# Attention value products: one accumulator over two banks in 64x32 tiles of TensorE, in place of two accumulators in 128x32 tiles

## What is computed

```python
q = (x @ Wq.T + bq).reshape(B, M, H, dqk)      # B 8, M 1024, H 8, dqk 2
k = (x @ Wk.T + bk).reshape(B, M, H, dqk)
v = (x @ Wv.T + bv).reshape(B, M, H, dv)       # dv 16
scores = jnp.einsum('bmhd,bnhd->bhmn', q, k) / math.sqrt(dqk)
scores = jnp.where(scores >= 0, scores, 0.2 * scores)
beta = jax.nn.softmax(scores, axis=-1)
out = jnp.einsum('bhmn,bnhd->bmhd', beta, v).reshape(B, M, C)
```

## Time and profile before

| | |
|---|---|
| median of three runs | 942.72 us |
| lowest, highest | 940.2 us, 944.03 us |
| span of the profiled execution, first to last instruction | 940.0 us |
| PE matmuls, busy | 861.2 us (92%) |
| DVE, busy | 735.3 us (78%) |
| ACT, busy | 691.3 us (74%) |
| GpSimd, busy | 601.5 us (64%) |
| granted TensorE clock, mean | 0.981 of full |

### The profile page before, as it was taken

How to read it: one execution, slowest core, us unless ns; L and a number is a source line. 1 busy time by engine, 2 the same in 40 slices (tenths; PEclk the granted TensorE clock), 3 DMA queues, 4 the chain that set the end, 5 groups by cost and what they waited for, 6 DMA issues and landing times. The chain is left out here.

```text
span 940.0 us, 20061 instructions
## 1 busy us (share of the span) xinstructions
PE 861.2 (92%) x7499; PEld 348.9 (37%) x7500; DVE 735.3 (78%) x859; ACT 691.3 (74%) x811; POOL 601.5 (64%) x610
## 2 busy tenths in 40 slices
PE   0688269999999999999999999999999999999997
PEld 0444112222222224776867732222222222222222
DVE  5788889999999994101011099999999999999996
ACT  0578888888888887444453568888888888888886
POOL 3355247777777663999999226657567575765782
PEclk9999659999999999999999999999999999999999
DMA  7833101111111112233242210102112111210202
GB/s 214 303 66 74 32 27 33 51 40 51 47 27 36 25 38 88 90 121 116 93 138 71 94 44 22 40 19 59 36 25 59 25 36 29 70 29 13 69 18 55
DMA packets 71225, 59.36 MB, mean 63 GB/s; under 512 B 33770, under 2 KB 58178, under 8 KB 71136
## 3 DMA queue, kind: packets, MB, share of 16 engines
q1 hardware_dynamic: 61520, 48.06, 17.6%
q0 software_dynamic: 8192, 9.37, 3.6%
q10 hardware_dynamic: 1424, 0.76, 0.3%
HBM read 31.58 MB, written 30.02 MB: 66 GB/s over the span
## 5 line engine op out<-in xcount | busy, mean ns | idle before, releaser
L1133 DVE TENSOR_SCALAR ps<-ps 128x1024 f32<-128x1024 f32 x512 | 600.1, 1224 | 14.6 <-PE ps L825 11.7
L718 ACT ACTIVATE pr<-ps 128x1024 f32<-128x1024 f32 x512 | 523.4, 1023 | 104.5 <-PE ps L835 72.9
L855 PE MATMUL ps<-pr,vp 128*32 128x256 f32 x4096 | 327.2, 392 | 0.1
L835 PE MATMUL ps<-q,kz 64*128 64x512 bf16 x1024 | 200.7, 389 | 10.2 <-DVE ps L1133 4.4
L825 PE MATMUL ps<-q,kz 62*128 62x512 bf16 x1024 | 200.3, 389 | 2.9 <-DMA q<-parts_dram 1.3
L505 POOL DMA_INDIRECT xs<-eout,idxs x128 | 129.0, 1008 | 105.0 <-ACT pr L718 75.5
L490 POOL DMA_INDIRECT disp<-xn,idx x128 | 125.9, 984 | 50.8 <-issue 29.2
L835 PEld LDWEIGHTS ps<-q,kz 64*128 64x128 bf16 x1024 | 49.0, 93 | 225.7 <-DVE ps L1133 188.4
L1152 DVE TENSOR_TENSOR pr<-ps,parts 128x1024 f32<-128x1024 f32 x12 | 14.7, 1225 | 149.6 <-PE ps L920 149.6
L855 PEld LDWEIGHTS ps<-pr,vp 128*32 128x32 f32 x4096 | 81.1, 108 | 119.4 <-issue 117.6
L744 ACT ACTIVATE pr<-ps,b1s 128x512 f32<-128x512 f32 x96 | 65.8, 687 | 53.7 <-PE ps L909 53.7
(11 more groups left out here) (122 smaller groups left out, 530.3 us busy)
## 6 DMA issues: line engine op xcount, KB each, us to landing
moved<-att SPq DMA_DIRECT2D x480, 8.0 KB
disp<-pr SPq DMA_DIRECT2D x12, 512.0 KB, 4.9
eout<-pr SPq DMA_DIRECT2D x12, 512.0 KB, 2.9
y<-in_x SPq DMA_DIRECT2D x8, 512.0 KB, 8.1
out<-y SPq DMA_DIRECT2D x7, 512.0 KB
w<-in_w1t SPq DMA_DIRECT2D x12, 256.0 KB, 3.2
w<-in_w2t SPq DMA_DIRECT2D x12, 256.0 KB, 3.4
xs<-disp SPq DMA_DIRECT2D x6, 512.0 KB, 4.9
```

What stands on the lines that cost most here:

```text
L718: act.activation(pr[:, c % BUFS, 2 * pair:2 * pair + 2, :], ring[i % RING], ACT.Exp, scale=SLOPE).then_inc(S["exps"], 1)
L835: last = pe.matmul(ring[i % RING][:, k, :], kz[r:r + TILE, hg, pair, kc * P:(kc + 1) * P], q2[r:r + TILE, hg, qh * HALF:(qh + 1) * HALF], ...
L855: last = pe.matmul(acc[p % 2][32 * g:32 * g + 32, cols], vp[:, hg, kc, g, :], pr[:, c % BUFS, g % PAIRS * 2 + g // PAIRS, cols], start=(kc ...
L1133: dve.tensor_scalar(s, s, 0.0, 1.0 / SLOPE - 1.0, ALU.max, ALU.mult).then_inc(S["relu"], 1)
```

## The change

The value products go over two row tiles. `values(m)` is called once for each unit as before, but it now issues eight matmuls in tiles of 64 rows and 32 columns: four heads for keys 0 to 63 of the block, and four heads for keys 64 to 127. The two row tiles work on different halves of the columns, and so write into different banks: the lower keys into the bank of half `m % 2`, the upper keys into the other one; the next call takes the crossed halves. The accumulator is therefore one for all passes, half of each of banks 6 and 7 (256 columns each). `pv` counts every call, and the counts of the waits on it are doubled. Every call waits for the one before it (`pv` of m), and the first call of pass p waits until pass p - 1 (not p - 2) is turned. TURN goes from 5 to 4. `scores` and `shifted` keep their 64x128 tiles. The PE's transposes at the end of a stretch go into `out_t`, the whole of bank 6.

```diff
-TURN = 5
+TURN = 4
...
-        acc = [ps[:, 2 * RING + k, :] for k in range(2)]
+        acc = ps[:, 2 * RING:2 * RING + 2, 0:HALF // 2]
+        out_t = ps[:, 2 * RING, :]
...
-                act.copy(ot[:, p % 2, :], acc[p % 2]).then_inc(S["acc_evac"], 1)
+                act.copy(ot[:, p % 2, :].rearrange("p (a q) -> p a q", a=2), acc).then_inc(S["acc_evac"], 1)
...
-            def values(c, half):
+            def values(m):
+
+                c, half = divmod(m, PAIRS)
 
                 p, kc = divmod(c, TB)
                 hg = p // NQ % NHG
-                cols = slice(half * HALF // 2, (half + 1) * HALF // 2)
-                pe.wait_ge(S["exps"], PAIRS * (c + 1))
+                if half == 0:
+                    pe.wait_ge(S["exps"], PAIRS * (c + 1))
+
+                wait_done(pe, "pv", PAIRS * c + half)
...
-                    wait_done(pe, "turned", p - 1)
-                for g in range(HG):
-                    last = pe.matmul(acc[p % 2][32 * g:32 * g + 32, cols], vp[:, hg, kc, g, :],
-                                     pr[:, c % BUFS, g % PAIRS * 2 + g // PAIRS, cols],
-                                     start=(kc == 0 and half == 0), stop=(kc == TB - 1), tile_position=(0, 32 * g),
-                                     skip_group_check=True)
-                if half:
-                    last.then_inc(S["pv"], 1)
+                    wait_done(pe, "turned", p)
+                for k in range(2):
+                    r, a = TILE * k, (k + half) % 2
+                    cols = slice(a * HALF // 2, (a + 1) * HALF // 2)
+                    for g in range(HG):
+                        last = pe.matmul(acc[32 * g:32 * g + 32, a, :], vp[r:r + TILE, hg, kc, g, :],
+                                         pr[r:r + TILE, c % BUFS, g % PAIRS * 2 + g // PAIRS, cols],
+                                         start=(kc == 0 and half == 0), stop=(kc == TB - 1),
+                                         tile_position=(r, 32 * g), skip_group_check=True)
+                last.then_inc(S["pv"], 1)
...
-                dve.wait_ge(S["pv"], TB * (p + 1))
+                dve.wait_ge(S["pv"], UP * (p + 1))
                 if p > 1:
                     dve.wait_ge(S["att_rdy"], quotients(p - 2))
-                dve.transpose(ot[:, p % 2, :], acc[p % 2]).then_inc(S["turned"], 1)
+                dve.transpose(ot[:, p % 2, :].rearrange("p (a q) -> p a q", a=2), acc).then_inc(S["turned"], 1)
```

More of the change, by code:

```diff
@@ L365, in _ @@
             spread(BH * NPB - 2)
-            sp.wait_ge(S["pv"], BH * NPB * TB)
+            sp.wait_ge(S["pv"], BH * NPB * UP)
             load_expert(1, 1)
@@ L425, in value_rows @@
                 if b > 0:
-                    pool.wait_ge(S["pv"], TB * (pass_at(b - 1, hg, NQ - 1) + 1))
+                    pool.wait_ge(S["pv"], UP * (pass_at(b - 1, hg, NQ - 1) + 1))
                 pool.tensor_copy(vp[:, hg, :, :, 0:DV1],
@@ L706, in evacuate @@
             def evacuate(p):
-                act.wait_ge(S["pv"], TB * (p + 1))
+                act.wait_ge(S["pv"], UP * (p + 1))
                 act.wait_ge(S["att_rdy"], quotients(p - 2))
-                act.copy(ot[:, p % 2, :], acc[p % 2]).then_inc(S["acc_evac"], 1)
+                act.copy(ot[:, p % 2, :].rearrange("p (a q) -> p a q", a=2), acc).then_inc(S["acc_evac"], 1)
             def exponentials(i):
@@ L716, in exponentials @@
                 if pair == 0:
-                    wait_done(act, "pv", c - BUFS + 1)
+                    wait_done(act, "pv", PAIRS * (c - BUFS + 1))
                 act.activation(pr[:, c % BUFS, 2 * pair:2 * pair + 2, :], ring[i % RING], ACT.Exp, scale=SLOPE
@@ L751, in ready @@
                 act.activation(kmax[:], gam[:], function, scale=0.0)
-            act.wait_ge(S["pv"], BH * NPB * TB - 1)
+            act.wait_ge(S["pv"], BH * NPB * UP - PAIRS)
             take_turned(0)
@@ L865, in turn @@
                 for t in range(GT):
-                    last = pe.transpose(acc[p % 2][:, t * P:(t + 1) * P], ot[:, p % 2, t * P:(t + 1) * P], ident)
+                    last = pe.transpose(out_t[:, t * P:(t + 1) * P], ot[:, p % 2, t * P:(t + 1) * P], ident)
                 last.then_inc(S["o_rdy"], 1)
@@ L880, in attention @@
                     if i > first + PAIRS:
-                        values((i - 3) // PAIRS, (i - 3) % PAIRS)
-                values((end - 3) // PAIRS, (end - 3) % PAIRS)
+                        values(i - 3)
+                values(end - 3)
                 if b1 == BH:
@@ L885, in attention @@
                     turn_rows(0, 0)
-                for j in range(end - 2, end):
-                    values(j // PAIRS, j % PAIRS)
+                for m in range(end - 2, end):
+                    values(m)
             def turn_rows(e, u):
@@ L1119, in finish @@
                 dve.wait_ge(S["o_rdy"], 1 + LAST.index(p))
-                rows = acc[p % 2].rearrange("p (t g c) -> p g t c", g=HG, c=BLOCK)
+                rows = out_t.rearrange("p (t g c) -> p g t c", g=HG, c=BLOCK)
                 inv_rows = rg[:, p % 2, :].rearrange("p (g t) -> p g t", g=HG)
```

## The result

The changed kernel takes 973.96 us (median of 4 runs, 972.25 to 975.66); the kernel before, run beside it, 942.61 us (4 runs). The ratio is 1.0345, with a 95% interval of 1.0327 to 1.0363: 31 us slower, where 26 were forecast (969 for 942.7). The profiled executions have spans of 940.0 and 970.4 us; that of the changed kernel is the fastest of its four runs.

What follows compares the result with a forecast made beforehand. A two-unit loop over ACT and PE of 2.40 us bounds the kernel; 6.9 + 19.5 + 0.9 = 27.3 us over 940.0 gives 967, 970 as median, forecast 969 us. Its own range is 957 to 982, widened to 934 to 985.

Steps and rivals of the forecast that it cites:

- The bound: Mid-pass attention: a loop over ACT and PE, 2.40 us for two units, sets the pace; neither PE nor DVE is full.
- The eight tiles, +6.9: Calls of values: four more tiles' stagger ends each call 0.027 us later, 256 times, +6.9 us; bounds 4 and 14.
- The tile shape on PE, 0: Switches between scores, values and shifted: about 0.09 us for changed columns stays unchanged, so 0.
- the first rival: Switches around values: no drain between tiles of the same rows, loop 2.24 us, about 935 us in all; chance 0.12.
- The turn, +19.5: Turn one unit earlier: DVE stands 0.7 us for the last values; 0.65 us lost at each of 30 turns, +19.5 us.
- in the loop of 2.40: After shifted(6), behind the turn: both kernels run the same two-unit loop of 2.40 us from there.
- PE's wait on turned: First values of a pass: PE's new wait needs 0.6 us, but is hidden behind rectify of unit 4.
- The pv waits, +0.9: Every call waits for the one before: costs 0.3 us where two calls stand back to back, three times, +0.9 us.
- The sum: Whole kernel: 6.9 + 19.5 + 0.9 = 27.3 us over the profiled span of 940.0.
- the stagger's room below: Eight tiles' stagger has more room below than above its size, so the forecast went from 970 to 969 us.
- The serial row tiles: Values: lower four tiles start only after the upper ones' first pass, call grows 0.24 us, about 1040 us; chance 0.10.
- The late turn: Turn on DVE: standing for the last values was forecast; the rival that it is not late gave about 950 us, chance 0.08.

Runs made afterwards that it cites:

- Run 7: The kernel before, with values streaming 128 of the 256 columns of each half, leaving out half of the queries' value products: 923.60 us.
- run 2: The kernel before with TURN = 4 and one accumulator, tiles still 128x32: 962.75 us, ratio 1.0215.
- run 9: Changed kernel, scores and shifted also in 64x32 tiles, ACT copying the accumulator to SBUF, DVE transposing from there before unit 5: 942.29 us, ratio 0.9998.
- run 5: The changed kernel (TURN = 4) with scores and shifted cut into 64x32 tiles too: 951.11 us, ratio 1.0100.
- run 6: The changed kernel with scores and shifted cut into 64x32 tiles too, and TURN = 5: 954.87 us, ratio 1.0137.
- run 1: The kernel before with TURN = 4 and nothing else, so 128x32 tiles and two accumulators: 965.02 us, ratio 1.0237.
- Run 8: The kernel before with pv counted by every call of values and every call waiting for the one before it: 942.01 us, ratio 1.0012.
- run 3: The changed kernel with TURN = 5: 972.49 us, ratio 1.0318.
- run 10: As run 9, but with DVE's transposition in front of unit 6: 943.96 us, ratio 1.0017.
- run 11: The changed kernel, scores in 64x128 tiles, with ACT copying the accumulator and DVE transposing from SBUF before unit 5: 957.13 us, ratio 1.0160.

## Why the prediction was right

**The bound.** Right. Run 7 shows it from below (a shorter call gives 18 us and then stops at DVE's 18.83 a pass), the changed kernel from above: the loop went from 2.40 to 2.42.

**The eight tiles, +6.9.** The mechanism was right. The last of the eight tiles starts 0.047 us after the first, where the last of four starts 0.020 after it: 0.027 later, as forecast. The loop grew by 0.023, 256 x 0.023 = 5.9 us. But tiles and waits together cost 10.1 us by the medians, where 7.8 were forecast, and 0.29 us more from turn to turn than in run 2 (20.44 for 20.16). Eight loops of 0.023 are 0.19 of that. Another 0.04 lies at the turn, which starts 0.11 us after the shown end of the last values where run 2 has 0.07. The rest is uneven: mid-pass loops of up to 2.66 us, where none exceeded 2.46 before, and the late releases counted at run 9. The forecast had no term for these.

**The tile shape on PE, 0.** Right: 0.32 from scores to values stayed. Runs 5 and 6 show that the price is paid for the change of columns, so the first rival falls for the reason that the prediction gave.

**The turn, +19.5.** Right in its mechanism, and 2 us low. Run 2, which has the turn's loss and not the tiles, takes 20.16 us from turn to turn in the mean for 19.43: 0.73 a turn where 0.65 was forecast, 21.8 us for 30, and 21.2 by the medians. The link that was too short is the one behind shifted(6). Up to there the forecast is close: its own steps give 216.03 - 215.40 = 0.63 (it went on with 0.65), and from the last values of a pass to shifted(6) run 2 takes 5.01 us at every turn for 4.41 before, 0.60 more. From there, the prediction says, both kernels are in the loop of 2.40. They are, but not at the same place in it. The loop has a short and a long step from shifted to shifted. In the kernel before, shifted(6) is followed by the short one, 1.14, and in run 2 by the long one, 1.26:

```profile
215.40 0.39 PE L835 MATMUL ps<-q,kz 64*128 64x512 bf16 x2
...
216.54 0.39 PE L835 MATMUL ps<-q,kz 64*128 64x512 bf16 x2
```

```profile
216.66 0.39 PE L835 MATMUL ps<-q,kz 64*128 64x512 bf16 x2
...
217.80 0.39 PE L835 MATMUL ps<-q,kz 64*128 64x512 bf16 x2
...
219.06 0.39 PE L835 MATMUL ps<-q,kz 64*128 64x512 bf16 x2
```

(the kernel before from shifted(6) to (7); run 2, shifted(5) to (7).) It is thirteen steps from shifted(6) to shifted(3) of the next pass, six loops and one step more: 15.59 us before, 15.72 in run 2, the missing 0.13. DVE stood as long as forecast. PE's wait on turned was said to be hidden; runs 1 and 2 show it. A smaller slip: in the changed kernel the turn starts 0.11 us after the last value matmul's shown end, where I took 0.05, and rectify(3) to turn is 1.9 for 1.8.

**The pv waits, +0.9.** Run 8 has 0.6 us of medians and 0.4 of span, inside its noise, in which 0.9 lies too. In mid-pass they are free: the loop is 2.40 as before.

**The sum.** By the medians 31.4 us: 21.2 for the turn (19.5 forecast) and 10.1 for tiles and waits (7.8); by the spans 30.4 for 27.3. Both terms came out some 2 us above their sizes, and within the bounds given for them. I had also taken 1 us off for the stagger's room below, which was the wrong way.

**The rivals.** The serial row tiles didn't come: sixteen matmuls take 0.66. The late turn came at every turn on DVE: 30 waits, 21.7 us in the changed kernel.

## What to carry to other kernels

Find the loop from start to start before trusting busy shares: here PE and DVE showed 99% and neither was full; a loop through PE and ACT was the bound. An operation that waits on one engine and is waited for by another needs a gap between producer and next user that is as long as its own time, and where the two follow at once, moving it earlier or later only chooses who stands; a copy by an engine with slack shortens the gap. And before an accumulator is shared to fit a tile shape, look at what the old one hid: in this order of calls the second accumulator was worth some 20 us (run 3 less the tiles' 10) without ever showing as a wait.

## What the runs showed of the hardware

- Going from 64x128 to 64x32 tiles costs about 0.1 us over the stream of the matmuls (0.32 against 0.22 from scores to values), though the rows stay, and going back about as much (0.60 against 0.43 from values to shifted, less 0.04 within the call). With eight small matmuls for two large ones, scores still take 0.41 us for 0.39.
- Eight tiles of 64x32 run two f32 passes over 256 columns in 0.66 us, where four of 128x32 take 0.64. From tile to tile the starts are 0.007 us apart in both; in run 5, where the matmuls in front have the same shape, 0.0035.
- The transposition of 128x512 f32 shows 0.717 us when DVE had to wait for it and 0.705 when not. From one bank it is 0.717 in runs 1 and 2 and 0.706 in the kernel before, from two banks 0.717 in the changed kernel and 0.705 in run 3.
- PE's next values start 0.85 us after the start of the transposition that they wait for, which is shown with 0.70 (run 3, all 30 turns), and 0.73 after the start of ACT's copy of the same 128x512 f32, shown with 0.58 (runs 9, 10 and 11).
- In the kernels with 40,800 instructions ACT at times starts long after the shown end of the PE matmuls that release it (0.07 us as a rule, 1.37 at the latest, in run 10); in the changed kernel, with 28,507, up to 0.36. No run here tells why.
